# Narrow gate matmuls in four groups between the products of the next batch's first stage, and a wait per half ahead of the transposes

## The chip, the cores and the metric

The kernel runs on one core of one Trainium2 chip. The metric is the device time of one execution, in microseconds (us). The program has two parts on that core: an attention part over eight batches, and after it a mixture-of-experts part. The change touches the first part alone.

## The reference

Input `x` is 8 batches of 1024 rows of 256 values. In short:

```python
x = x + layernorm(attn(layernorm(x)))     # q, k, v from one projection; scores = q k^T / 4 over 1024 keys,
                                          # softmax, times v; out = swapaxes + reshape, then w_proj + bias
x = x + layernorm(ffn(layernorm(x)))
# ffn: logits = xn2 @ gate_w.T; scores = softmax(logits); top 1024 rows for each of 16 experts,
#      gated MLP of each expert (256 -> 1024 -> 256), weighted scatter-add, plus a shared MLP (256 -> 512 -> 256)
```

`xn2`, the second normalised rows, feeds the gate (16 logits for each row) as well as the experts.

## The kernel before

**Rounds.** The attention part is a loop over rounds r = 0 to 9, written out for each engine. Round r does the attention of batch r (r < 8), the output projection and first residual of batch r-1 (`R.post`, 1 to 8), and the gate of batch r-2 (`R.gate`, 2 to 9). Rounds 3 to 6 are a hardware loop; the others are written out. Each engine runs its own list in order, and semaphores couple them, so the written order is the order of the work.

**TensorE in a round.** The list of one round from 2 to 7 is:

1. Transposes of the normalised rows `XNB` of batch r-2 into the four PSUM banks of `psS` (L284). Sixteen of them, in four groups k = 0 to 3. Groups 0 and 1 read the rows of the first half (`ht` = 0, four tiles of 128 rows), groups 2 and 3 those of the second. Ahead of all of them stands one wait for both halves (`s_xn2`).
2. The output projection Y of batch r-1, 48 matmuls of 256 columns, 12 to a bank. It waits for the last `O_lo` of the round before (`s_ol`), and each bank for ScalarE's copy of its transposes (`s_n2`).
3. The gate's logits (L309): 16 calls of 16 columns, full fp32, which the trace shows as 32 matmuls, all into `psL`.
4. The first stage of batch r, in the code's name `tT`: x times the 256x256 matrix that joins the query and key weights. Four banks of six matmuls of 512 columns (three for each product, since operands are split into a high and a low part). One wait ahead of it asks for all four of VectorE's bias additions that empty the banks of Y (`s_yb`).
5. V (48 matmuls of 256 columns), and then eight steps of scores, transposes of the probabilities (L358) and outputs.

**ScalarE.** In the last step of a round it normalises tiles 4 to 7 into `XNB` (`norm_x1(r, range(4, 8))`, L391), and only then scales the last output tile (`O_hi`, L470), from which VectorE makes `O_lo` (L599). Tiles 0 to 3 are normalised one and two steps earlier. The half's semaphore `s_xn2` rises at tiles 3 and 7. At the start of the next round ScalarE copies the transposes (`xn2T`, L430).

**VectorE** adds the bias to Y (L522), then makes the low parts of `tT` and V, and then reads the logits (`gate_shift`, L538).

Of the kernel before, what the change touches and what calls it, by code (L numbers as in the profile page):

```python
# [31 lines left out]
NB, S, D = 8, 1024, 256  # L32
# [6 lines left out]
NT = S // P  # L39
# [9 lines left out]
def wait(eng, sem, value):  # L49

    if isinstance(value, int) and value <= 0:
        return
    eng.wait_ge(sem, value)


def mm3(pe, out, w_hi, w_lo, x_hi, x_lo, first, last):

    pe.matmul(out, w_hi, x_hi, start=first, stop=False)  # L58
    pe.matmul(out, w_hi, x_lo, start=False, stop=False)  # L59
    return pe.matmul(out, w_lo, x_hi, start=False, stop=last)  # L60
# [101 lines left out]
def attention(nc, io, c):  # L162
    with ExitStack() as ctx:
# [31 lines left out]
        s_y, s_yb = sem("s_y"), sem("s_yb")  # L195
        s_tr2, s_n2 = sem("s_tr2"), sem("s_n2")
        s_lg = sem("s_lg")
# [3 lines left out]
        s_pv, s_oh, s_ol = sem("s_pv"), sem("s_oh"), sem("s_ol")  # L201

        s_r1, s_xn, s_ry, s_yn, s_x1, s_r2, s_xn2 = (sem(n) for n in ("s_r1", "s_xn", "s_ry", "s_yn", "s_x1", "s_r2", "s_xn2"))
        s_sm, s_sme, s_sc = sem("s_sm"), sem("s_sme"), sem("s_sc")
# [4 lines left out]
        def output_bank(i):  # L209
            return (psO, psL)[i % 2][:, 0:D]  # L210
# [49 lines left out]
        def _(pe):  # L260
            def turn_x(b, ks):
                for k in ks:
                    dk, ht = k % 2, k // 2
                    if dk == 0:
                        wait(pe, s_xn, 2 * b + ht + 1)
                    for j in range(4):
                        i = pe.transpose(psS[:, k, j * P:(j + 1) * P], xn[:, 4 * ht + j, dk * P:(dk + 1) * P], c.ident[:, :])
                    i.then_inc(s_tr, 1)
# [6 lines left out]
            def body(R):  # L275
                r = R.r
                if R.gate:
                    wait(pe, s_xn2, 2 * (r - 1))
                    for k in range(4):
                        dk, ht = k % 2, k // 2  # L280
                        if R.attn:
                            wait(pe, s_xl, 4 * r + k + 1)
                        for j in range(4):
                            i = pe.transpose(psS[:, k, j * P:(j + 1) * P], XNB[:, 4 * ht + j, dk * P:(dk + 1) * P], c.ident[:, :])  # L284
                        i.then_inc(s_tr2, 1)
                if R.post:

                    wait(pe, s_ol, 8 * r)
                    for k in range(4):
# [5 lines left out]
                        for jj in range(2):  # L295
                            for q in range(2):
                                ot = 2 * (2 * jp + jj) + q
                                i = mm3(pe, psS[:, k, jj * D:(jj + 1) * D],
                                        O[0][:, ot, hm * P:(hm + 1) * P], O[1][:, ot, hm * P:(hm + 1) * P],
                                        c.wp[0][:, q, :], c.wp[1][:, q, :], q == 0, q == 1)  # L300
                        i.then_inc(s_y, 1)
                if R.gate:

                    wait(pe, s_n2, 4 * (r - 1))
                    wait(pe, s_sm, r - 2)
                    wait(pe, s_ol, 8 * r if R.attn else 8 * NB)
                    for t in range(NT):
                        for k in range(KD):
                            i = pe.matmul(psL[:, t * E:(t + 1) * E], xn2T[:, k, t * P:(t + 1) * P], c.gw[:, k, :],  # L309
                                          start=(k == 0), stop=(k == KD - 1))  # L310
                    i.then_inc(s_lg, 1)
                if R.attn:
                    wait(pe, s_xl, 4 * (r + 1))
                    if R.post:
                        wait(pe, s_yb, 4 * r)
                    for k in range(4):
                        m, h = k % 2, k // 2
                        for kk in range(KD):
                            w = [c.m[z][:, kk, m * P:(m + 1) * P] for z in (0, 1)]
                            x = [xnT[z][:, kk, h * 512:(h + 1) * 512] for z in (0, 1)]  # L320
                            i = mm3(pe, psS[:, k, :], w[0], w[1], x[0], x[1], kk == 0, kk == KD - 1)
                        i.then_inc(s_tt, 1)
                if R.attn:
                    for k in range(4):
                        wait(pe, s_tl, 4 * r + k + 1)
                        for t2 in range(2):
                            t = 2 * k + t2
                            for kk in range(KD):
                                w = [xnT[z][:, kk, t * P:(t + 1) * P] for z in (0, 1)]
                                i = mm3(pe, psS[:, k, t2 * D:(t2 + 1) * D], w[0], w[1],  # L330
                                        c.wv[0][:, kk, :], c.wv[1][:, kk, :], kk == 0, kk == KD - 1)
                        i.then_inc(s_v, 1)
                    for step in range(NT + 2):
                        i0, i1, i2 = step, step - 1, step - 2
                        if i0 < NT:
                            b = 2 * (i0 % 2)
                            if i0 < 2:
                                wait(pe, s_vl, 4 * r + 2 * i0 + 2)
                            else:
                                wait(pe, s_exp, 8 * r + i0 - 1)  # L340
                            for n in range(2):
                                for kk in range(KD):
                                    w = [tT[z][:, kk, i0 * P:(i0 + 1) * P] for z in (0, 1)]
                                    x = [xnT[z][:, kk, n * 512:(n + 1) * 512] for z in (0, 1)]
                                    i = mm3(pe, psS[:, b + n, :], w[0], w[1], x[0], x[1], kk == 0, kk == KD - 1)
                            i.then_inc(s_s, 1)
                        if R.ln_next and i0 >= NT:
                            if i0 == NT:
                                wait(pe, s_exp, 8 * r + 7)
                                turn_x(r + 1, (0, 1))  # L350
                            else:
                                wait(pe, s_exp, 8 * r + 8)
                                turn_x(r + 1, (2, 3))
                        def turn_p():
                            wait(pe, s_exp, 8 * r + i1 + 1)
                            wait(pe, s_ptl, 2 * (8 * r + i1))
                            for t in range(NT):
                                i = pe.transpose(psPT[:, t * P:(t + 1) * P], Pr[:, i1 % 2, t * P:(t + 1) * P], c.ident[:, :])  # L358
                                if t % 4 == 3:
                                    i.then_inc(s_t, 1)  # L360

                        def output(ts):
                            if ts[0] == 0:
                                wait(pe, s_ptl, 2 * (8 * r + i2 + 1))
                                wait(pe, s_ol, 8 * r + i2 - 1)
                                if i2 == 1 and R.gate:
                                    wait(pe, s_sm, r - 1)
                                if i2 == 0:
                                    wait(pe, s_vl, 4 * (r + 1))
                            for t in ts:  # L370
                                i = mm3(pe, output_bank(i2), PT[0][:, i2 % 2, t, :], PT[1][:, i2 % 2, t, :],
                                        V[0][:, t, :], V[1][:, t, :], t == 0, t == NT - 1)
                            if ts[-1] == NT - 1:
                                i.then_inc(s_pv, 1)

                        if i0 == NT:
                            output(range(NT // 2))
                            turn_p()
                            output(range(NT // 2, NT))
                        else:  # L380
                            if 0 <= i1 < NT:
                                turn_p()
                            if i2 >= 0:
                                output(range(NT))
            rounds(pe, body)

        @blk.scalar
# [1534 lines left out]
```

## Time and profile before

| | us |
|---|---|
| time before, median of 3 runs | 2126.94 (2126.02 to 2127.23) |
| the profiled execution's own time | 2126.23 |
| its span, first to last instruction | 2124.4 |
| TensorE matmul, busy | 2038.0 (96%) |
| VectorE, busy | 1194.5 (56%) |
| ScalarE, busy | 972.0 (46%) |
| mean granted TensorE clock | 0.981 |

Matmuls overlap one another in the trace: a matmul of 256 columns is shown with 0.28 us, and yet the next starts 0.12 us later. So lengths of stretches are read from start to start. "Idle before" in brackets is the time in which the engine had nothing under way.

### The profile page before, as it was taken

The page shows a single profiled execution, that of the slowest core. Times are in us where ns is not written, and L with a number is a line of the kernel's source. Part 1 is how long each engine was busy: PE and PEld are TensorE (multiplying, and loading weights), DVE is VectorE, ACT ScalarE, POOL GpSimd, SP SyncE. Part 2 cuts the span into 40 slices and gives each one's busy share as a digit, 9 for nine tenths or more (in the row PEclk, how much of TensorE's full clock was granted, in tenths as well). Part 3 has the DMA queues.
Part 4 walks back from the last instruction along what each step waited for, and adds up shares of the span by engine and source line. Part 5 has one row for each costly group of instructions (what it writes and reads, how often), then busy time and mean ns, then how long its engine had stood idle before and what let it go on. Part 6 is the DMA issues. An engine that isn't in the chain of part 4 may idle for free.

```text
span 2124.4 us, 32679 instructions
## 1 busy us (share of the span) xinstructions
PE 2038.0 (96%) x12590; PEld 1819.0 (86%) x12592; DVE 1194.5 (56%) x2518; ACT 972.0 (46%) x1809; POOL 436.3 (21%) x450
## 2 busy tenths in 40 slices
PE   7999999999994998999999999999999999999996
PEld 6899998998994887788888888888889898988885
DVE  5586686586564776555464546443443435353565
ACT  4464564564552433444343434344443434443443
POOL 0000000000001000212223222323233322322255
PEclk9999999999996999999999999999999999999998
DMA  3011110110014211233333333333333333334266
GB/s 112 1 41 42 60 62 41 59 60 41 40 42 159 102 60 42 69 91 91 61 91 62 91 64 88 64 89 71 83 79 77 76 80 84 69 91 100 53 193 132
DMA packets 55557, 159.91 MB, mean 75 GB/s; under 512 B 9473, under 2 KB 25985, under 8 KB 48257
## 3 DMA queue, kind: packets, MB, share of 16 engines
q1 hardware_dynamic: 28912, 116.16, 15.2%
q0 software_dynamic: 26512, 41.96, 12.4%
q8 instruction: 87, 1.43, 0.3%
q14 instruction: 46, 0.37, 0.1%
HBM read 98.78 MB, written 59.31 MB: 74 GB/s over the span
## 4 chain that ended last, share of the span: by engine, by line
PE 63%; DVE 2%; POOL 1%; ACT 1%; issue 1%; another core or an unknown queue 0%; DMA 0%; DVEq 0%; SPq 0%; ACTq 0%; POOLq 0%
PE mo_psD L58 7%; PE mo_psD L59 7%; PE mo_psD L60 7%; PE mo_psG L58 7%; PE mo_psU L60 7%; PE mo_psU L58 7%; PE mo_psG L59 7%; PE mo_psG L60 7%; PE mo_psU L59 7%; PE mo_psX L1210 1%; PE mo_psX L1026 1%; DVE mo_st L1502 0%; POOL mo_rs L1792 0%; DVE mo_HF L1538 0%
## 5 line engine op out<-in xcount | busy, mean ns | idle before, releaser
L1538 DVE TENSOR_TENSOR mo_HF<-mo_psU,mo_HF 128x512 f32<-128x512 f32 x320 | 221.0, 691 | 646.7 <-ACT mo_HF L1379 623.2
L1379 ACT ACTIVATE mo_HF<-mo_psG 128x512 f32<-128x512 f32 x320 | 191.2, 598 | 478.4 <-PE mo_psU L60 430.4
L1764 POOL DMA_INDIRECT ACC<-mo_OUT,mo_GI x128 | 202.9, 1585 | 700.1 <-ACT mo_OUT L1446 691.4
L60 PE MATMUL mo_psD<-mo_wd_hi,mo_H_lo 128*128 128x256 f32 x1024 | 289.8, 283 | 0.0
L59 PE MATMUL mo_psD<-mo_wd_lo,mo_H_hi 128*128 128x256 f32 x1024 | 289.8, 283 | 0.0
L58 PE MATMUL mo_psD<-mo_wd_hi,mo_H_hi 128*128 128x256 f32 x1024 | 289.6, 283 | 0.0
L1483 DVE TENSOR_TENSOR mo_H_lo<-mo_HF,mo_H_hi 128x512 fp32r<-128x512 f32 x300 | 204.3, 681 | 0.0
L1357 ACT ACTIVATE mo_H_hi<-mo_HF 128x512 fp32r<-128x512 f32 x320 | 199.7, 624 | 1.0 <-DVE mo_HF L1538 1.0
L59 PEld LDWEIGHTS mo_psD<-mo_wd_lo,mo_H_hi 128*128 128x128 f32 x1024 | 196.5, 192 | 1.2
L58 PEld LDWEIGHTS mo_psD<-mo_wd_hi,mo_H_hi 128*128 128x128 f32 x1024 | 196.5, 192 | 1.2
L60 PEld LDWEIGHTS mo_psD<-mo_wd_hi,mo_H_lo 128*128 128x128 f32 x1024 | 196.5, 192 | 0.0
L1446 ACT ACTIVATE mo_OUT<-mo_psD,mo_TW 128x256 f32<-128x256 f32 x128 | 60.7, 474 | 277.5 <-PE mo_psD L60 275.1
L654 POOL TENSOR_TENSOR X<-X,X1a 128x1024 f32 (+1 forms) x15 | 36.4, 2424 | 618.7 <-ACT X1a L391 618.7
L58 PE MATMUL mo_psG<-mo_XT_hi,wg_hi 128*128 128x512 f32 x344 | 140.3, 408 | 11.0 <-DVE mo_XT_lo L1478 11.0
L1753 POOL DMA_INDIRECT mo_XG<-XN,mo_GI x128 | 128.1, 1001 | 48.0 <-issue 34.1
L58 PE MATMUL mo_psU<-mo_XT_hi,wu_hi 128*128 128x512 f32 x344 | 135.4, 393 | 0.0
L59 PE MATMUL mo_psG<-mo_XT_lo,wg_hi 128*128 128x512 f32 x344 | 134.9, 392 | 0.0
L60 PE MATMUL mo_psG<-mo_XT_hi,wg_lo 128*128 128x512 f32 x344 | 134.7, 392 | 0.0
L60 PE MATMUL mo_psU<-mo_XT_hi,wu_lo 128*128 128x512 f32 x344 | 134.4, 391 | 0.0
L59 PE MATMUL mo_psU<-mo_XT_lo,wu_hi 128*128 128x512 f32 x344 | 134.4, 391 | 0.0
L58 PE MATMUL mo_psG<-mo_XT_hi,mo_wg_hi 128*128 128x512 f32 x280 | 113.0, 403 | 1.3 <-DVE mo_HF L1538 0.9
L59 PE MATMUL mo_psG<-mo_XT_lo,mo_wg_hi 128*128 128x512 f32 x280 | 109.3, 390 | 0.0
(262 smaller groups left out, 5183.3 us busy)
## 6 DMA issues: line engine op xcount, KB each, us to landing
X1a<-wg_in SPq DMA_DIRECT2D x16, 1024.0 KB, 4.9
X1a<-wu_in SPq DMA_DIRECT2D x16, 1024.0 KB, 4.9
X1a<-wd_in SPq DMA_DIRECT2D x16, 1024.0 KB, 4.9
XN<-XNB SPq DMA_DIRECT2D x8, 1088.0 KB, 4.1
X<-x_in SPq DMA_DIRECT2D x8, 1024.0 KB, 6.1
out_dram<-X SPq DMA_DIRECT2D x8, 1024.0 KB, 4.4
XN2T<-xn2T SPq DMA_DIRECT2D x8, 1024.0 KB, 3.8
mo_F<-ACC SPq DMA_DIRECT2D x7, 1024.0 KB, 12.8
```

The source lines that it names most:

```text
L58: pe.matmul(out, w_hi, x_hi, start=first, stop=False)
L59: pe.matmul(out, w_hi, x_lo, start=False, stop=False)
L60: return pe.matmul(out, w_lo, x_hi, start=False, stop=last)
L654: g.tensor_tensor(x, x, Y[:, 4 * h:4 * h + 4, :], ALU.add).then_inc(s_x1, 1)
L1026: i = pe.matmul(self.ps[:, 0, 0:SL * GE], self.lo1[:, t, :, :].rearrange("p v e -> p (v e)"), self.val[:, :, t * GE:(t + 1) * GE], start=( ...
L1357: a.activation(H[0][:, slot(b, it), :], HF[:, it % 2, :], ACT.Copy).then_inc(s_hhi, 1)
L1379: a.activation(HF[:, it % 2, :], psG[:, it % 2, :], ACT.Gelu).then_inc(s_gelu, 1)
L1446: a.activation(OUT[:, t, :], psD[:, t % 2, 0:D], ACT.Copy, scale=scale).then_inc(s_ev, 1)
L1483: v.tensor_tensor(H[1][:, z, :], HF[:, it % 2, :], H[0][:, z, :].bitcast(F32), ALU.subtract).then_inc(s_hlo, 1)
L1538: v.tensor_tensor(HF[:, it % 2, :], psU[:, it % 2, :], HF[:, it % 2, :], ALU.mult).then_inc(s_mul, 1)
L1753: g.indirect_dma_start(out=XG[q][:, t, :], out_offset=None, in_=io["XN"], in_offset=bass.IndirectOffsetOnAxis(ap=GI[q][:, t:t + 1], axis=0 ...
L1764: g.indirect_dma_start(out=io["ACC"], out_offset=bass.IndirectOffsetOnAxis(ap=GI[n % 2][:, 4 * tb + t:4 * tb + t + 1], axis=0), in_=OUT[:, ...
```

## The change

In rounds 2 to 7 the logits leave their place between Y and the first stage. They are issued in four groups of four calls (eight matmuls in the trace), one group behind each bank of the first stage. Their semaphores are waited for ahead of the first group, and `s_lg` rises behind the last. Rounds 8 and 9, which have no first stage, keep the logits in one piece.

The first stage waits for VectorE's bias additions bank by bank, in every round from 1 to 7. The transposes wait for `s_xn2` at each group: one half for groups 0 and 1, both for groups 2 and 3. In rounds 8 and 9 they wait for both halves as before.

```diff
@@ TensorE, body(R)
                 if R.gate:
-                    wait(pe, s_xn2, 2 * (r - 1))
                     for k in range(4):
                         dk, ht = k % 2, k // 2
+                        wait(pe, s_xn2, 2 * (r - 2) + ht + 1 if R.attn else 2 * (r - 1))
                         if R.attn:
                             wait(pe, s_xl, 4 * r + k + 1)
...
-                if R.gate:
-
-                    wait(pe, s_n2, 4 * (r - 1))
-                    wait(pe, s_sm, r - 2)
-                    wait(pe, s_ol, 8 * r if R.attn else 8 * NB)
-                    for t in range(NT):
+                def logits(ts):
+
+                    if ts[0] == 0:
+                        wait(pe, s_n2, 4 * (r - 1))
+                        wait(pe, s_sm, r - 2)
+                        wait(pe, s_ol, 8 * r if R.attn else 8 * NB)
+                    for t in ts:
                         for k in range(KD):
                             i = pe.matmul(psL[:, t * E:(t + 1) * E], xn2T[:, k, t * P:(t + 1) * P], c.gw[:, k, :],
                                           start=(k == 0), stop=(k == KD - 1))
-                    i.then_inc(s_lg, 1)
+                    if ts[-1] == NT - 1:
+                        i.then_inc(s_lg, 1)
+
+                if R.gate and not R.attn:
+                    logits(range(NT))
                 if R.attn:
                     wait(pe, s_xl, 4 * (r + 1))
-                    if R.post:
-                        wait(pe, s_yb, 4 * r)
                     for k in range(4):
                         m, h = k % 2, k // 2
+                        if R.post:
+                            wait(pe, s_yb, 4 * (r - 1) + k + 1)
                         for kk in range(KD):
                             w = [c.m[z][:, kk, m * P:(m + 1) * P] for z in (0, 1)]
                             x = [xnT[z][:, kk, h * 512:(h + 1) * 512] for z in (0, 1)]
                             i = mm3(pe, psS[:, k, :], w[0], w[1], x[0], x[1], kk == 0, kk == KD - 1)
                         i.then_inc(s_tt, 1)
+                        if R.gate:
+                            logits((2 * k, 2 * k + 1))
```

On TensorE, in the hardware loop (rounds 3 to 6), between the last matmuls of Y and the first stage, the program before has this. Each `psL<-gw,xn2T` row is a call of 16 columns, and `psS<-xnT_hi,m` the first stage.

```order
1319 L60 MATMUL psS<-wp,O_lo 128x256
1320 L53 REGISTER_ALU
1321 L309 MATMUL psL<-gw,xn2T 128x16 [waits s_ol,s_sm,s_n2]
1322 L309 MATMUL psL<-gw,xn2T 128x16 x15
1323 L53 ISA
1324 L58 MATMUL psS<-xnT_hi,m 128x512 [waits s_yb,s_xl]
1325 L59 MATMUL psS<-xnT_lo,m 128x512
```

The changed program has this in the same place.

```order
1323 L60 MATMUL psS<-wp,O_lo 128x256
1324 L53 ISA
1325 L53 ISA [waits s_xl]
1326 L58 MATMUL psS<-xnT_hi,m 128x512 [waits s_yb]
...
1331 L60 MATMUL psS<-xnT_hi,m 128x512
1332 L310 MATMUL psL<-gw,xn2T 128x16 [waits s_ol,s_sm,s_n2]
1333 L310 MATMUL psL<-gw,xn2T 128x16 x3
1334 L53 REGISTER_ALU
1335 L58 MATMUL psS<-xnT_hi,m 128x512 [waits s_yb]
...
1341 L310 MATMUL psL<-gw,xn2T 128x16 x4
1342 L53 REGISTER_ALU
1343 L58 MATMUL psS<-xnT_hi,m 128x512 [waits s_yb]
```

The sixteen calls that stood in a row ahead of the first stage are now four pieces, and the first stage follows on Y directly.

On TensorE, at the start of the loop's body, the transposes of `XNB` stand like this before.

```order
1255 L53 ISA [waits s_xn2]
1256 L284 MATMUL psS<-ident,XNB 128x128 [waits s_xl]
1257 L284 MATMUL psS<-ident,XNB 128x128 x3
1258 L53 REGISTER_ALU
1259 L284 MATMUL psS<-ident,XNB 128x128 [waits s_xl]
1260 L284 MATMUL psS<-ident,XNB 128x128 x3
```

And they stand like this in the changed program.

```order
1258 L53 ISA [waits s_xn2]
1259 L284 MATMUL psS<-ident,XNB 128x128 [waits s_xl]
1260 L284 MATMUL psS<-ident,XNB 128x128 x3
1261 L53 REGISTER_ALU [waits s_xn2]
1262 L284 MATMUL psS<-ident,XNB 128x128 [waits s_xl]
1263 L284 MATMUL psS<-ident,XNB 128x128 x3
1264 L53 REGISTER_ALU
1265 L53 REGISTER_ALU [waits s_xn2]
1266 L284 MATMUL psS<-ident,XNB 128x128 [waits s_xl]
```

The transposes keep their order, and the wait for `s_xn2` has gone from one to four, each with a register operation ahead of its group.

## Rows read from the trace of the kernel before

**Rows 1.** The page: busy time, and the granted clock in 40 equal slices.

```profile
PE 2038.0 (96%) x12590; PEld 1819.0 (86%) x12592; DVE 1194.5 (56%) x2518; ACT 972.0 (46%) x1809; POOL 436.3 (21%) x450
...
PEclk9999999999996999999999999999999999999998
```

**Rows 2.** TensorE's waits, 0 to 1000 us: total us, times, longest.

```profile
PE psS L284 <- ACT XNB L391: 21.9, 7, 18.1
...
PE mo_psG L58 <- DVE mo_XT_lo L1478: 11.0, 1, 11.0
...
PE psS L58 <- DVE X1a L522: 0.9, 1, 0.9
```

**Rows 3.** Stretches: busy of PE, PEld, DVE, ACT, POOL; granted clock; DMA.

```profile
250.60:254.00 3.40, 3.40 (x34) 3.40 (x32) 0.69 (x1) 0.00 (x0) 0.00 (x0) 1.00 0.02 5
254.90:258.10 3.20, 3.20 (x9) 2.52 (x8) 0.69 (x1) 0.60 (x1) 0.00 (x0) 0.50 0.00 0
...
910.20:913.50 3.30, 3.30 (x18) 3.30 (x17) 1.96 (x4) 0.38 (x1) 0.00 (x0) 0.50 0.00 0
```

**Rows 4.** Timeline, TensorE, round 3: start, length, instruction, idle before.

```profile
242.26 0.28 PE L60 MATMUL psL<-V_hi,PT_lo 128*128 128x256 f32 x1
243.03 1.96 PE L284 MATMUL psS<-ident,XNB 128*128 128x128 f32 x16 [0.49 <-ACT XNB L391]
244.75 0.36 PE L58 MATMUL psS<-wp,O_hi 128*128 128x256 f32 x1
...
250.59 3.64 PE L309 MATMUL psL<-gw,xn2T 128*128 128x16 f32 x32
254.08 0.47 PE L58 MATMUL psS<-xnT_hi,m 128*128 128x512 f32 x1
...
255.31 0.63 PE L59 MATMUL psS<-xnT_lo,m 128*128 128x512 f32 x1
255.74 0.63 PE L60 MATMUL psS<-xnT_hi,m 128*128 128x512 f32 x1
...
261.26 0.28 PE L58 MATMUL psS<-wv,xnT_hi 128*128 128x256 f32 x1
```

**Rows 5.** Timeline, TensorE, round 1, which has no gate.

```profile
96.96 0.28 PE L60 MATMUL psS<-wp,O_lo 128*128 128x256 f32 x1
98.11 0.47 PE L58 MATMUL psS<-xnT_hi,m 128*128 128x512 f32 x1 [0.87 <-DVE X1a L522]
98.42 0.40 PE L59 MATMUL psS<-xnT_lo,m 128*128 128x512 f32 x1
...
103.66 0.28 PE L58 MATMUL psS<-wv,xnT_hi 128*128 128x256 f32 x1
```

**Rows 6.** Timeline, TensorE, round 7: logits, and the start of V.

```profile
565.69 3.98 PE L309 MATMUL psL<-gw,xn2T 128*128 128x16 f32 x32
...
576.34 0.28 PE L58 MATMUL psS<-wv,xnT_hi 128*128 128x256 f32 x1
```

**Rows 7.** Timeline, TensorE, a score step: transposes of probabilities between wide matmuls.

```profile
355.15 1.04 PE L358 MATMUL psPT<-ident,Pr 128*128 128x128 f32 x8
355.94 0.36 PE L58 MATMUL psO<-V_hi,PT_hi 128*128 128x256 f32 x1
356.15 0.27 PE L59 MATMUL psO<-V_lo,PT_hi 128*128 128x256 f32 x1
```

**Rows 8.** Timeline, TensorE, start of round 5: last output, first transpose.

```profile
399.62 0.28 PE L60 MATMUL psL<-V_hi,PT_lo 128*128 128x256 f32 x1
400.65 0.54 PE L284 MATMUL psS<-ident,XNB 128*128 128x128 f32 x3 [0.75 <-ACT XNB L391]
```

**Rows 9.** Timeline, ScalarE, the same place.

```profile
398.49 2.03 ACT L391 ACTIVATE XNB<-X,shift,rs 128x256 f32 x4
400.43 0.45 ACT L470 ACTIVATE O_hi<-psL,rinv 128x256 fp32r<-128x256 f32 x1
```

**Rows 10.** Timeline, VectorE, the same place.

```profile
400.91 0.48 DVE L599 SCALAR_TENSOR_TENSOR O_lo<-psL,rinv,O_hi 128x256 fp32r<-128x256 f32 x1 [1.00 <-ACT O_hi L470]
```

## Prediction

> **What bounds the kernel now.** I read the page first: TensorE is busy 96% of the span and the next engine 56% [rows 1], so time can only come out of TensorE's own stretch, out of its pauses and out of its clock. Then TensorE's waits. Three of them lie where the change works or behind it: 21.9 us in seven pauses ahead of the transposes of `XNB`, of which 18.1 is one pause; and 0.9 us ahead of the first stage in round 1 [rows 2]. The pause of 18.1 is that of round 9, behind the last projection, where the code still waits for both halves; so the six rounds 2 to 7 share 3.8 us. The 11.0 us at the start of the expert part wait for a chain that begins when attention has ended [rows 2].
>
> Then the table of stretches, for the clock. In 250.60 to 254.00 TensorE is busy in every microsecond, with 34 matmuls, nearly all logits, and the clock is at its upper level (1.00, 2.4 GHz). In 254.90 to 258.10, at the start of the first stage, it is at the lower (0.50, 1.2 GHz) [rows 3]. The same table gives 0.50 right behind the logits in all six rounds 2 to 7, 78.5 us apart. The digits of the clock on the page are blind to it [rows 1]: a slice is 53 us long and such a low stretch a small part of it.
>
> Last, the timeline, from start to start. In round 3 the logits run from 250.59 to 254.08 (3.49 us) and the first stage from there to 261.26 (7.18 us), together 10.67. Low matmuls of 512 columns start 0.43 us apart (255.31, 255.74) [rows 4]. In round 1, which has no logits, the same 24 matmuls take from 98.11 to 103.66, 5.55 us, at the upper level [rows 5]. So 10.67 stand against 3.49 + 5.55 = 9.04: the fall costs 1.63 us a round. In round 7 the pair takes 576.34 - 565.69 = 10.65 [rows 6]; the other four lie between 10.63 and 10.67.
>
> **First part: the logits in four groups.** No instruction goes and none comes. What changes is how long TensorE does nothing but matmuls of 16 columns: 3.49 us in one piece before, four pieces of about 0.9 us with 1.4 us of wide matmuls (5.55 / 4) between them now. The reading is that the clock falls because for 3.4 us TensorE is busy with matmuls that stream hardly any columns. Two things in the trace speak for it: there is no pause ahead of the fall at all, and it comes only behind the logits, not behind the sixteen transposes of 128 columns (243.03 to 244.75), which have a real pause of 0.49 us in front of them [rows 4] and less narrow work in a row. A piece of 0.9 us is half of that transposing stretch, so I expect the upper level to hold. Gain: 6 x 1.63 = 9.8 us, less in rounds where a little of it is the switch below; I take 9.7. Its ends are 0 (the falls stay) and 9.8.
>
> The Trainium skill, "TensorE: Matmul & The Clock Gate", section "Why this matters for your kernels", advises against idle gaps between bursts of matmuls, since the clock goes back behind one. By that rule a stretch without a pause holds the upper level and the logits would have cost nothing; the trace shows the fall behind a stretch that is busy throughout [rows 3], so here the measurement decides.
>
> What does the splitting cost? A switch from narrow to wide delays the second wide matmul: 0.31 us from 98.11 to 98.42 where 0.23 is usual, so 0.08. Against that a group's first narrow matmuls come sooner. The nearest piece of the same size is that of eight transposes in a score step: 0.79 us until the next wide matmul, which is followed after 0.21 us instead of 0.12 [rows 7], so 0.88 for eight, 0.110 each. The logits in one piece cost 3.49 + 0.08 = 3.57 for 32, 0.112 each. Four groups of 0.88 are 3.52. I put the splitting at 0; its ends are -0.05 and, if every one of three new switches costs 0.08 with nothing given back, +0.25 a round, 1.5 us in all.
>
> **Second part: the bank's own bias wait.** In rounds 2 to 7 the logits covered the wait for the last bias addition (0.69 us of VectorE). Now the first stage follows on Y directly, but bank 0 needs only the first addition, three projections old (4.3 us), and bank 3 comes after three banks and three groups, some 6.8 us on. No wait is left. In round 1 there was no cover: last matmul of Y at 96.96, first stage at 98.11, where 97.08 would have been the next start. That is 1.03, and with the late second matmul 1.11 us [rows 5]. I take 1.1; ends 0.9 (the idle time alone) and 1.1.
>
> **Third part: the transposes.** In round 3 the last output matmul starts at 242.26 and the first transpose at 243.03, where 242.38 was due: 0.65 lost, shown as 0.49 idle [rows 4]. In round 5 it is 400.65 against 399.74: 0.91 [rows 8]. Idle time plus 0.16 is the loss, so the six rounds lose 3.8 + 6 x 0.16 = 4.8 us. Now groups 0 and 1 start at once, since the first half was normalised two steps earlier; they take half of 1.72, 0.86 us.
>
> What is late next? In round 5, the worst, ScalarE's rows end at 400.52 (398.49 + 2.03) and TensorE saw them at 400.65; groups 2 and 3 would be due at 399.74 + 0.86 = 400.60, so they start at 400.65 and end at 401.51 [rows 8, 9]. Y then waits for the last `O_lo`. `O_hi` stands behind those rows on ScalarE and ends at 400.88 [rows 9], `O_lo` ends at 401.39 [rows 10], and with the 0.13 us that TensorE took to see ScalarE's rows it may start at 401.52. Before, Y started at 400.65 + 1.72 = 402.37. So 0.85 of 0.91 comes back in rounds 4 to 6, and all of it in the other three, where the pause is shorter: 4.8 - 3 x 0.06 = 4.6 us. The two waits behind the one removed are level with it; were `O_lo` visibly later, it would cap this. Ends: 0 and 4.8.
>
> The added waits and their register operations stand in TensorE's queue, with everything of the round behind them. Y has four such waits now: its 48 matmuls take 250.59 - 244.75 = 5.84, which is 48 x 0.12 plus the 0.08 of the switch [rows 4]. So a wait that is already met costs 0.
>
> **Behind these places.** The last logits end 5.5 us later than before (9.04 - 3.49), but VectorE reads them only after the low parts of V, which end later still, so `gate_shift` doesn't wait. Rounds 8 and 9 are as before. Everything from there on hangs on the end of attention through TensorE, VectorE and DMAs in series, so what attention gains I pass on in full. The expert part has its own low stretches, behind its own pauses; one is 910.20 to 913.50 [rows 3]. Which matmuls such a stretch catches can shift with the start of the part, and I allow 1.6 us either way for each of two.
>
> **Sum.** 9.7 + 1.1 + 4.6 = 15.4 us. The profiled execution took 2126.2 us (span 2124.4 and 1.8 around it), so 2110.8. The median of the runs is 0.7 above that execution: 2111.5 us, 0.7% faster.
>
> **Rivals.**
>
> *The clock still falls in some or all rounds.* The narrow work is as much as ever, and over the stretch of 9 us it is still 40% of the time. For: nothing in the trace shows exactly this mix. Against: the score steps mix 0.8 us of transposes with wide work and stay up, though these have 128 columns and not 16. All six falls kept: 2126.9 - 1.1 - 4.6 = 2121.2; one to three kept: 2113 to 2116.4. Chance 15%.
>
> *Another wait takes the place of that for `XNB`.* `O_lo` is level with it to a few hundredths in round 5; if ScalarE's copies of the transposes or `O_lo` end later than read here, the 4.6 go: 2116.1. Chance 6%.
>
> *The slower end: each narrow group pulls the clock down, and the whole first stage runs at the lower level.* Place: the first stage of rounds 2 to 7. Price: 24 matmuls at 0.43 are 10.3 us instead of 5.55, with the narrow pieces 13.8 against 10.65 now, so +3.2 a round, +19.2, less the 5.7 of the other parts: 2140. It turns slower than before as soon as a round pays over 0.95 us (5.7 / 6) beyond today's fall. Against it stands that the wide matmuls between groups outlast the groups. Chance 4%.
>
> The Trainium skill, "TensorE: Matmul & The Clock Gate", section "A second HAM failure mode: psum-queue depth-cycling", speaks for this rival: frequent tiny pauses between groups made one kernel's clock swing back and forth. No row here shows it, and the score steps of this kernel with their short breaks don't.
>
> **How the numbers follow.** Forecast 75%, some falls kept 15%, the other wait 6%, slower 4%. A difference within 0.2% (4.3 us) is about what a measurement of this kernel can't tell from no change. All cases but the slower one, and a small part of the kept falls that adds up with another loss, end over 0.2% faster: faster 94%, same 3%, slower 3%. The range goes from 2107.5 (everything at its upper end, and both low stretches of the expert part gone) to 2118 (four falls kept, or the third part lost and one stretch of the expert part dearer).
>
> **What would show it.** Right: clock 1.00 throughout the rounds 2 to 7; logits and first stage together about 9.1 us in each; no pause ahead of the transposes over 0.1 us; no 0.87 us in round 1; the only large wait for `XNB` still that of 18 us. Wrong: 0.50 anywhere in a first stage, a new wait of Y for `O_lo` or `xn2T`, or gains that stand at the end of attention and are gone at the end of the span.

## The result

| | before | changed |
|---|---|---|
| median | 2127.09 us (4 runs, 2126.02 to 2128.38) | 2113.75 us (4 runs, 2111.77 to 2114.11) |
| profiled execution, own time | 2126.23 | 2114.11 |
| its span | 2124.4 | 2112.3 |
| ratio of the runs | | 0.9935, 95% interval 0.9918 to 0.9952 |

The changed kernel is 13.3 us faster by the medians, 12.1 us in the profiled pair. 2111.5 was forecast, in a range of 2107.5 to 2118.

### The profile page after: what moved, and what is told of

Its sections match the earlier page's. It is cut to its first block, busy times and chain, and to the rows that moved or that the text cites. A ratio compares the mean times of both kernels' runs of the same rounds, so it can differ in the third digit from the quotient of the medians.

```text
span 2112.3 us, 32697 instructions
## 1 busy us (share of the span) xinstructions
PE 2030.2 (96%) x12590; PEld 1814.4 (86%) x12592; DVE 1195.0 (57%) x2518; ACT 971.2 (46%) x1809; POOL 436.1 (21%) x450
## 3 DMA queue, kind: packets, MB, share of 16 engines
q1 hardware_dynamic: 28912, 116.16, 15.3%
## 4 chain that ended last, share of the span: by engine, by line
PE 64%; DVE 2%; issue 1%; POOL 1%; ACT 1%; DVEq 0%; another core or an unknown queue 0%; ACTq 0%; POOLq 0%
PE mo_psD L58 7%; PE mo_psD L60 7%; PE mo_psD L59 7%; PE mo_psG L58 7%; PE mo_psU L58 7%; PE mo_psG L59 7%; PE mo_psG L60 7%; PE mo_psU L60 7%; PE mo_psU L59 7%; PE mo_psX L1217 1%; PE mo_psX L1033 1%; DVE mo_st L1509 0%; POOL mo_rs L1799 0%; DVE mo_HF L1545 0%; DVE mo_XT_lo L1485 0%
```

## The profile after

The page of the changed kernel: busy time and the digits of the clock.

```profile
PE 2030.2 (96%) x12590; PEld 1814.4 (86%) x12592; DVE 1195.0 (57%) x2518; ACT 971.2 (46%) x1809; POOL 436.1 (21%) x450
...
PEclk8999999999995999999999999999999999999998
```

The same number of matmuls, 8 us less of busy time. As before [rows 1], the digits hide what happened in the rounds. The mean granted clock is 0.981 in both profiled executions, although six low stretches are gone; the reader should ask where others have come in. The stretches table of the changed kernel (busy of PE, PEld, DVE, ACT, POOL; clock; DMA) shows first two of the six stretches from the start of the first stage to V, then round 9's logits and the expert part's first matmuls.

```profile
170.60:179.60 9.00, 9.00 (x58) 7.95 (x57) 2.77 (x4) 2.38 (x4) 0.00 (x0) 1.00 0.00 0
247.30:256.30 9.00, 9.00 (x58) 7.96 (x56) 2.77 (x4) 2.37 (x4) 0.00 (x0) 1.00 0.01 2
...
654.10:657.50 3.40, 3.40 (x17) 3.40 (x17) 0.00 (x0) 0.00 (x0) 0.00 (x0) 0.50 0.73 308
657.50:660.80 3.30, 3.30 (x17) 3.30 (x16) 0.00 (x0) 0.00 (x0) 0.00 (x0) 0.50 0.00 0
672.00:675.90 3.90, 3.88 (x9) 3.11 (x10) 0.00 (x0) 0.46 (x1) 3.87 (x67) 0.50 1.08 414
```

The first two answer to [rows 3]: 1.00 where 0.50 stood, and the other four rounds read the same. The third and fourth are new in kind: all of round 9's logits at the lower level, 17 matmuls in 3.4 us against 34 in the same time at the upper [rows 3].

The second new place is the start of the program, ahead of everything that was changed. Round 0's first matmuls, before and then changed:

```profile
21.30:27.30 6.00, 6.00 (x17) 4.71 (x18) 0.82 (x2) 1.20 (x2) 0.00 (x0) 1.00 0.00 1
```

```profile
21.40:27.40 6.00, 6.00 (x14) 4.73 (x15) 0.69 (x1) 1.12 (x2) 0.00 (x0) 0.50 0.01 1
```

The changed kernel's timeline on TensorE in round 3 (start, length) is the answer to [rows 4].

```profile
239.66 0.28 PE L60 MATMUL psL<-V_hi,PT_lo 128*128 128x256 f32 x1
239.79 1.91 PE L284 MATMUL psS<-ident,XNB 128*128 128x128 f32 x16
241.45 0.36 PE L58 MATMUL psS<-wp,O_hi 128*128 128x256 f32 x1
...
247.29 0.40 PE L58 MATMUL psS<-xnT_hi,m 128*128 128x512 f32 x1
...
248.68 0.96 PE L310 MATMUL psL<-gw,xn2T 128*128 128x16 f32 x8
249.49 0.49 PE L58 MATMUL psS<-xnT_hi,m 128*128 128x512 f32 x1
249.81 0.40 PE L59 MATMUL psS<-xnT_lo,m 128*128 128x512 f32 x1
...
256.33 0.36 PE L58 MATMUL psS<-wv,xnT_hi 128*128 128x256 f32 x1
```

The transposes start 0.13 us behind the last output, without a pause. From the first stage to V it is 256.33 - 247.29 = 9.04 us, against 10.67. A group of eight takes 0.81 us to the next wide matmul, which is followed after 0.32.

In round 5 ScalarE's timeline

```profile
391.32 2.03 ACT L398 ACTIVATE XNB<-X,shift,rs 128x256 f32 x4
393.26 0.45 ACT L477 ACTIVATE O_hi<-psL,rinv 128x256 fp32r<-128x256 f32 x1
```

VectorE's

```profile
393.74 0.48 DVE L606 SCALAR_TENSOR_TENSOR O_lo<-psL,rinv,O_hi 128x256 fp32r<-128x256 f32 x1 [0.99 <-ACT O_hi L477]
```

and TensorE's

```profile
392.57 2.00 PE L284 MATMUL psS<-ident,XNB 128*128 128x128 f32 x16
394.36 0.38 PE L58 MATMUL psS<-wp,O_hi 128*128 128x256 f32 x1
```

answer to [rows 8 to 10]. `O_lo` ends at 394.22 (393.74 + 0.48) and Y starts at 394.36, 1.79 us behind the first transpose (1.66 in round 3). So rounds 4 to 6 still lose 0.13 us each, and round 7 loses 0.11. Read one by one, the transposes show where: the ninth, the first of group 2, starts 0.91 us behind the first instead of 0.87, and the tenth 0.16 behind the ninth instead of 0.11, so 0.08 us lie at the wait for the second half of `XNB`. The other 0.05 lie at Y, where `O_lo` is the last to come. Neither is long enough to stand in the list of waits.

TensorE's waits of [rows 2], 0 to 1000 us, total, times, longest:

```profile
PE psS L284 <- ACT XNB L398: 18.1, 1, 18.1
PE mo_psG L58 <- DVE mo_XT_lo L1485: 11.0, 1, 11.0
```

The six pauses for `XNB` and the one in round 1 are gone; what was left alone by the change is as long as before.

## The experiments

The first four runs shared a chip and the kernel before beside them, and so did the next four and runs nine to eleven. Run 12 had a fourth chip. Beside runs 5 to 8 and 12 the kernel before takes 2120 us instead of 2126 to 2127. The difference is in the expert part: from its first matmul to the end 1432 to 1433 us on those two chips and 1437 to 1442 on the others. So times are compared by their ratio to the kernel before on the same chip, and attention by the length from the first stage of round 1 to the start of round 8, which is 536.5 us before (634.58 - 98.11) and 522.7 changed (620.44 - 97.74).

### 1. The wait per half alone

```diff
 (kernel before)
                 if R.gate:
-                    wait(pe, s_xn2, 2 * (r - 1))
                     for k in range(4):
                         dk, ht = k % 2, k // 2
+                        wait(pe, s_xn2, 2 * (r - 2) + ht + 1 if R.attn else 2 * (r - 1))
```

> The kernel before with the third part alone (a wait per half ahead of the transposes). My theory: the parts add up, so this one gives its 4.6 us (2122.5 us), no pause over 0.1 us is left ahead of the transposes of rounds 2 to 7, Y starts 0.57 to 0.85 us sooner, and the six falls of the clock stay. Rival, the wait for O_lo takes its place: a new pause ahead of Y and about 2127.

Measured: 2119.0 us beside 2126.8, ratio 0.9966 (0.9952 to 0.9979), 7.8 us and not 4.6. No pause is left ahead of the transposes in its waits. The stretches just behind the logits of rounds 2 to 7 in its profile (the fifth reads the whole first stage of round 6):

```profile
171.90:175.10 3.20, 3.20 (x24) 2.99 (x25) 0.00 (x0) 0.00 (x0) 0.00 (x0) 1.00 0.00 0
250.40:253.40 3.00, 3.00 (x9) 2.50 (x9) 0.00 (x0) 0.00 (x0) 0.00 (x0) 0.50 0.00 0
328.90:331.90 3.00, 3.00 (x9) 2.32 (x8) 0.02 (x1) 0.60 (x1) 0.00 (x0) 0.50 0.00 0
407.40:410.40 3.00, 3.00 (x9) 2.35 (x8) 0.69 (x1) 0.60 (x1) 0.00 (x0) 0.50 0.00 0
482.00:490.00 8.00, 8.00 (x49) 7.02 (x49) 1.93 (x3) 1.79 (x3) 0.00 (x0) 1.00 0.00 0
561.00:564.00 3.00, 3.00 (x8) 2.32 (x8) 0.00 (x0) 0.42 (x1) 0.00 (x0) 0.50 0.00 0
```

Four falls instead of six. In rounds 2 and 6 logits and first stage take 9.06 us, in the others 10.62 to 10.67. Two falls less are 3.2 us, and 4.6 + 3.2 = 7.8. So the part's own gain was read rightly, and that it leaves the clock alone was not: with the same piece of logits but rounds of another length, fewer rounds fell. The rival (a wait for `O_lo` of the same size in its place) is out.

### 2. The bank's own bias wait alone

```diff
 (kernel before)
-                    if R.post:
-                        wait(pe, s_yb, 4 * r)
                     for k in range(4):
                         m, h = k % 2, k // 2
+                        if R.post:
+                            wait(pe, s_yb, 4 * (r - 1) + k + 1)
```

> The kernel before with the second part alone (the first stage waits for the bias additions bank by bank). My theory: it acts in round 1 alone, since the logits cover it elsewhere: 1.0 to 1.1 us (2126.0), the pause of 0.87 us gone, the six falls kept. Rival, it gives more because the first stage also waits in rounds 2 to 7: over 2 us.

Measured: 2126.61, ratio 1.0004 (0.9994 to 1.0013). No gain over all. In the profile the pause of round 1 is gone and the first stage there follows Y after 0.12 us, so 1.1 us were won; but three stretches of it, in rounds 2, 3 and 7, read

```profile
174.00:180.00 6.00, 6.00 (x18) 4.94 (x18) 0.69 (x1) 0.60 (x1) 0.00 (x0) 0.50 0.00 0
255.80:258.90 3.10, 3.10 (x9) 2.42 (x8) 0.69 (x1) 0.60 (x1) 0.00 (x0) 0.50 0.02 5
570.00:576.00 6.00, 6.00 (x16) 4.80 (x16) 0.69 (x1) 0.73 (x2) 0.00 (x0) 0.50 0.00 0
```

In rounds 2 and 7 the low stretch is twice as long and logits and first stage take 12.2 to 12.3 us. Its ten runs lie between 2124.5 and 2130.7, which is nearly four such stretches (6.2 us). While the falls exist, a gain of 1 us drowns in how many there are and how long. That the spread of the ten runs comes from them is likely and not shown, since only one of the ten was profiled.

### 3. The changed kernel with one wait for both halves

```diff
 (changed kernel)
                 if R.gate:
+                    wait(pe, s_xn2, 2 * (r - 1))
                     for k in range(4):
                         dk, ht = k % 2, k // 2
-                        wait(pe, s_xn2, 2 * (r - 2) + ht + 1 if R.attn else 2 * (r - 1))
```

> The changed kernel with the old single wait for both halves ahead of the transposes, so the logits in groups and the bank's own bias wait. My theory: 9.7 + 1.1 = 10.8 us off (2116.3), no fall of the clock in rounds 2 to 7, 3.8 us of waits for XNB back. Rival, the groups need the shorter pause ahead of the transposes to hold the clock: falls come back in some rounds, 1.6 us each, up to 2126.

Measured: 2115.51, ratio 0.9941 (0.9928 to 0.9955), 11.3 us off where 10.8 were expected. Its waits have the six pauses back

```profile
PE psS L284 <- ACT XNB L398: 3.8, 6, 0.8
```

and every round has 9.04 us from Y to V, no fall. Attention takes 527.2 us, 4.5 more than the changed kernel. So in the changed kernel the wait per half is worth 4.5 us, while alone it was worth 7.8: the two falls that it saves by itself are saved already.

### 4. The changed kernel with one wait for all bias additions

```diff
 (changed kernel)
                     wait(pe, s_xl, 4 * (r + 1))
+                    if R.post:
+                        wait(pe, s_yb, 4 * r)
                     for k in range(4):
                         m, h = k % 2, k // 2
-                        if R.post:
-                            wait(pe, s_yb, 4 * (r - 1) + k + 1)
```

> The changed kernel with the old wait for all four bias additions ahead of the first stage. My theory: with the logits gone from in front of it, the wait stands bare in all seven rounds 1 to 7, about 1.1 us each, so 7.7 us slower than the changed kernel (2121.5), with a pause of 0.87 us in each and the clock still up. Rival, only round 1 pays: 2114.9.

Measured: 2120.07 beside 2126.8, ratio 0.9967 (0.9955 to 0.9978), 6.3 us over the changed kernel's 2113.75 where 7.7 were expected. TensorE's waits, 0 to 640 us:

```profile
PE psS L58 <- DVE X1a L529: 6.1, 7, 0.9
```

Seven pauses of 0.87 us, and from the end of Y (0.12 us behind the start of its last matmul) to V 10.12 us instead of 9.04. The wait that the logits had covered costs 1.08 us a round as soon as they leave, 6.5 in rounds 2 to 7 (attention 529.2 us against 522.7), and with round 1 the expected 7.6; the rival is out. The clock stays up in all six rounds. Compared with experiment 1, which has the third part alone, this kernel has the groups on top and is no faster (0.9967 against 0.9966, attention 529.2 against 528.6): four falls saved, six bare waits paid. So the second part, which gained nothing measurable alone, is what makes the first one pay here.

### 5. Two groups instead of four

```diff
 (changed kernel)
-                        if R.gate:
-                            logits((2 * k, 2 * k + 1))
+                        if R.gate and k % 2 == 1:
+                            logits(range(4 * (k // 2), 4 * (k // 2) + 4))
```

> The changed kernel with the logits in two groups of eight calls (behind banks 1 and 3) instead of four of four. My theory: a piece of 1.8 us with 2.8 us of wide matmuls between still holds the upper level, so Y's end to V stays 9.04 us in each round and the time within noise of the changed kernel (2112 to 2115). Rival, four groups were needed: 0.50 in some first stages, 1.6 us each, 2117 or more.

Measured: 2104.98 beside 2120.32, ratio 0.9926 (0.9910 to 0.9941). The clock reads 1.00 in all six rounds, each piece takes 1.70 us to the next wide matmul, Y to V takes 9.02 us and attention 522.5 (522.7 with four groups). As good as four groups.

### 6. One piece, in another place

```diff
 (changed kernel)
-                        if R.gate:
-                            logits((2 * k, 2 * k + 1))
+                        if R.gate and k == 3:
+                            logits(range(NT))
```

> The changed kernel with all logits in one piece behind bank 3, ahead of V. My theory: the piece of 3.5 us pulls the clock down wherever it stands, now in V, in most of the rounds (four of six in the kernel before with the half wait alone), 1.6 us each: 2119 to 2123. Rival, what mattered was the place (the wait for the bias additions, the first stage's operands) and not the length of the piece: no fall, 2114.

Measured: 2110.02 beside 2120.32, ratio 0.9946 (0.9930 to 0.9961), 0.2% over the run before it. The stretches behind the logits of rounds 2, 3 and 4, which are in V now:

```profile
179.00:182.00 3.00, 3.00 (x16) 3.00 (x15) 0.18 (x1) 0.60 (x1) 0.00 (x0) 0.50 0.03 5
257.50:260.50 3.00, 3.00 (x16) 3.00 (x16) 0.69 (x1) 0.60 (x1) 0.00 (x0) 0.50 0.00 0
333.90:337.00 3.10, 3.10 (x28) 3.10 (x28) 0.20 (x1) 0.60 (x1) 0.00 (x0) 1.00 0.00 0
```

Rounds 2, 3, 5 and 6 fall, 4 and 7 don't, and attention takes 528.1 us, 5.4 more than changed. So the place is not what matters: in V too the clock falls behind the unbroken piece of 3.5 us. The number of falls came as expected. The time came out better, 10.3 us under the kernel before where 4 to 8 were expected; experiment 5 on the same chip is 15.3 under it too, where the changed kernel's own comparison has 13.3, and that difference stays unexplained.

### 7. Groups of double size

```diff
 (changed kernel)
-                    for t in ts:
+                    for t in [t for t in ts for _ in range(1 + bool(R.attn))]:
```

> The changed kernel with each logit call of rounds 2 to 7 issued twice in its group (the second overwrites the sum with a doubled one, so the logits are not the reference's). Groups of sixteen narrow matmuls with 1.4 us of wide ones between, narrow work 56% of the time over 12.6 us. If the clock holds: 32 more at 0.112 in six rounds, 21.5 us, 2135. My theory: it holds in some rounds and falls in others, 2137 to 2145. Rival, any alternation with wide work is enough: 2135 and no 0.50.

Measured: 2125.0 beside 2120.32, ratio 1.0020 (1.0010 to 1.0029). No fall, against what I expected; two rounds in its profile:

```profile
170.00:184.00 14.00, 14.00 (x101) 12.96 (x100) 3.46 (x5) 2.39 (x4) 0.00 (x0) 1.00 0.00 1
250.00:264.00 14.00, 14.00 (x101) 12.96 (x100) 3.46 (x5) 2.39 (x4) 0.00 (x0) 1.00 0.00 0
```

All six rounds take 12.62 us from Y to V, 3.58 more than 9.04, so 0.112 us for each of 32 more matmuls, and attention 21.4 us more. So in this run the clock held although narrow work took more than half of the time, in pieces of 1.70 us with 1.4 us of wide work between them. The expectation misread the edit in one point: both calls of a repeated pair are made again, the first with `start` set, so the sum begins anew and the logits are the same as before, not doubled. The work on TensorE is what was intended.

### 8. Wide matmuls in round 9's pause

```diff
 (changed kernel)
+                if R.gate and not R.attn and not R.post:
+                    for n in range(72):
+                        pe.matmul(psPT[:, 0:512], xnT[0][:, 0, 0:P], xnT[0][:, 0, 0:512], start=True, stop=True)
                 if R.gate:
```

> The changed kernel with 72 matmuls of 512 columns in round 9's pause of 18 us ahead of the last transposes (into a bank of which nothing is read), so that TensorE is not idle there. My theory: the last transposes and logits run at the upper level, 1.5 us and 3.1 us shorter where they ran low in the profiled execution; all of it goes to the start of the expert part: 2109 to 2111, and less spread between runs. Rival, the chain to the expert part goes through DMAs and not through the logits: no change.

Measured: 2102.93 beside 2120.32, ratio 0.9916 (0.9902 to 0.9929). The last transposes and the last logits:

```profile
650.40:653.00 2.60, 1.87 (x17) 1.63 (x15) 0.00 (x0) 1.92 (x4) 0.00 (x0) 1.00 0.00 0
653.20:656.60 3.40, 3.40 (x31) 3.40 (x31) 0.00 (x0) 0.00 (x0) 0.00 (x0) 1.00 0.73 308
```

Upper level; transposes to logits 2.8 us instead of 4.4, logits 3.5 instead of 6.6 in the changed kernel's profile (start to start). From the start of round 8 to the first matmul of the expert part it takes 48.2 us instead of 51.6, although the 72 matmuls outlasted the pause by 1.4 us. The chain goes through the logits; the rival is out.

### 9. The changed kernel again

> The changed kernel once more, beside the next two on one chip, since the last four runs had another chip than the first five. Against the kernel before: ratio 0.9935 as before, within 0.9918 to 0.9952, and attention without a fall of the clock.

Measured: 2111.15 beside 2126.45, ratio 0.9929 (0.9915 to 0.9943), attention 522.7 us, no fall. Here the last logits took 4.1 us and the start of round 8 to the expert part 50.0 us instead of 51.6.

### 10 to 12. Both pauses filled, and an earlier load

```diff
 (changed kernel; 60 matmuls ahead of round 9's transposes, and n more here: 34, 30, 14)
                 if R.gate and not R.attn:
                     logits(range(NT))
+                if R.gate and not R.attn and not R.post:
+                    for n in range(34):
+                        pe.matmul(psPT[:, 0:512], xnT[0][:, 0, 0:P], xnT[0][:, 0, 0:512], start=True, stop=True)
...
 (SyncE, in 11 and 12)
+                if R.post and not R.attn:
+                    sp.wait_ge(s_xtst, 16)
+                    sp.dma_start(c.XR0[:, :, :], io["XN2T"][0][:, :, 0:512]).then_inc(c.s_xr0, 16)
...
-            sp.dma_start(c.XR0[:, :, :], io["XN2T"][0][:, :, 0:512]).then_inc(c.s_xr0, 16)
```

> The changed kernel with 60 wide matmuls in round 9's pause (72 outlasted it by 1.4 us in the last trial) and 34 more behind the last logits, ahead of the expert part. My theory: 4 to 6 us under the changed kernel from round 9, and another 2 to 3 us because the expert part's first twenty-four matmuls (5.2 us for the first twelve at the lower level) start at the upper one. Rival, the pause of some 3 us between the parts lets the clock fall all the same: only the first gain.

> The same (30 matmuls in the second place) with the load of XR0, which ends the attention part, issued in round 8 instead of behind the last store of XN. My theory: the barrier to the expert part then waits for that store alone, which landed 4.8 us after its issue where the load took until 6.1 us after it: 1.3 to 2 us less. Rival, the expert part's start hangs on something else: no change against the run beside it.

> The last kernel with 14 matmuls instead of 30 behind the last logits. In it SyncE was done at 663.8 us and the barrier between the parts still came at 666.5, because TensorE was working off the 30. My theory: the barrier now comes 2 to 2.7 us sooner, the expert part's first matmuls may run at the lower level (about 1.5 us back), and the sum is 0.5 to 2.5 us under the last two: ratio 0.991. Rival, the last run's gain was not hidden by these matmuls: same time or slower.

Measured: run 10, 2109.72 beside 2126.45, ratio 0.9922 (0.9909 to 0.9936); run 11, 2109.64, ratio 0.9920 (0.9906 to 0.9933); run 12, on its own chip, 2102.02 beside 2120.39, ratio 0.9915 (0.9901 to 0.9928). In run 10 the last logits and the expert part's first twelve matmuls read

```profile
651.90:653.60 1.70, 1.70 (x16) 1.70 (x16) 0.00 (x0) 0.00 (x0) 0.00 (x0) 1.00 0.62 265
653.80:656.70 2.90, 2.90 (x15) 2.90 (x16) 0.00 (x0) 0.00 (x0) 0.00 (x0) 0.50 0.43 181
669.00:671.80 2.80, 2.80 (x12) 2.34 (x13) 0.00 (x0) 0.42 (x1) 2.80 (x55) 1.00 1.04 398
```

The second filling did its work here (2.9 us for twelve, against 4.9 in run 9 and 5.2 in the kernel before), the first only in part: half way through the logits the clock is at the lower level. Run 10 is 1.4 us under run 9 by the medians, not the 6 us and more expected. In run 11, where 1.3 to 2 us more were expected and 0.1 measured, SyncE's waits show why the early load gave nothing:

```profile
SPq L258 <- DMA XN<-XNB: 3.7, 1, 3.7
SPq L163 <- PEq L163: 2.5, 1, 2.5
```

The store that is left made SyncE wait 3.7 us, and then SyncE stood 2.5 us at the barrier for TensorE, which was working off the 30 matmuls. The filling also missed its other aim there: with 30 matmuls instead of 34 the expert part's first twelve ran at the lower level again (clock 0.50 from 668.60 to 671.80) and took 4.3 us. With 14 (run 12) the start of round 8 to the expert part takes 45.6 us, against 48.6 in run 11 and 51.6 in the changed kernel's first profile. Runs 11 and 12 differ in nothing but these 16 matmuls, so that the barrier waited for them is shown. Run 12 has the lowest ratio of all, but its interval overlaps that of the changed kernel; that it is faster over all is likely and not settled.

## Why the prediction was right

**The mechanism and its size held.** First part: 9.04 us in each of six rounds against 10.63 to 10.67, 9.7 us, as forecast. Experiment 3 shows it without the third part; experiments 5 and 6 show that the length of the unbroken piece does it and not its place. Second part: 98.11 - 96.96 = 1.15 us in round 1 became 0.12, and the delayed second matmul went too: 1.1 us, as forecast. Third part: pause and transposes together became 0.6 to 0.8 us shorter in each round, 4.6 us in all, as forecast, and as read from [rows 8 to 10] the second half of `XNB` and `O_lo` came nearly level with the transposes: they still cost 0.08 and 0.05 us in the worst rounds.

**The splitting was mis-sized, within its bounds.** It was put at 0. V now stands behind narrow work: its 48 take 5.84 us instead of 5.75, so 0.09 in six rounds, 0.5 us.

**Two terms were missing, both outside the changed places.** The sum of the parts is 15.4 - 0.5 = 14.9 us, and round 8 starts 14.1 us sooner (620.44 against 634.58). Of the difference 0.7 us comes from the program's start: Y of round 1 begins 0.66 us later (91.89 against 91.23) ahead of anything that was changed, and 0.56 of it is round 0's first stage, 8.40 us with the lower level at its start instead of 7.84. And then 2.8 us were lost between round 9's logits and the expert part: 15.20 us from the first of these logits to the first expert matmul before, 18.00 changed. The prediction put rounds 8 and 9 "as before" and allowed only for the expert part's low stretches, 1.6 us either way for each of two; those came to 0.8 us in favour (1441.1 us before, 1440.3 changed). The larger term was round 9's logits, in one piece behind a pause of 18 us, which before ran mostly at the upper level. The stretch there, in the kernel before:

```profile
668.10:671.10 3.00, 2.97 (x27) 2.97 (x27) 0.00 (x0) 0.00 (x0) 0.00 (x0) 1.00 0.72 306
```

That is not a fixed cost of the change: run 9, the same kernel, has 15.5 us in that place, and experiment 2 (which has no group) has 18.0. Of the ten profiles with nothing added in round 9, three show 18.0 (the changed kernel, experiments 2 and 6) and seven 15.0 to 15.7. With the 15.2 of the kernel before the profiled execution would have taken 2111.3 us; 2110.8 was forecast for it. Run 9 stands at 2111.15, 15.3 us under the kernel before beside it. So part of the miss of 2.2 us in the median may be in which level these logits met; only one of the first four runs was profiled.

**The additive reading was wrong in one place.** The parts were priced apart and summed. In the sum this was harmless, since all three are made; taken alone they don't behave so (7.8, 0 and, for the first with the old bias wait, 6 x 1.08 us of it eaten). The tacit step that failed is that six falls come with the piece of 3.5 us: with the same piece and rounds of another length there were four (experiment 1). The groups alone, with both old waits, were not run.

**The rivals.** No fall stayed. The slower rival got nothing: groups of 8, of 16, and of 16 with half the wide work between them all read 1.00. Its price was too low as well. It let the narrow pieces keep their 3.5 us at the lower level, where round 9's logits took 6.6 (the same 32 matmuls), so such a round would have cost some 6 us more and not 3.2. The Trainium skill, "TensorE: Matmul & The Clock Gate", section "A second HAM failure mode: psum-queue depth-cycling", tells of tiny idle times between groups of matmuls; the groups here left none (busy 9.00 us of 9.00), so no run here tests it.

**What stays open.** What picks the rounds that fall, when one unbroken piece stands in each (four of six in experiments 1 and 6, all six before, and all six in experiment 2, two of them twice as long), was not tried further. Nor was it tried what in these matmuls does it: that they have only 16 columns was argued, and no run has an equally long piece of other matmuls. The four runs of the changed kernel differ by 2.3 us; from round 9's logits to the expert part the profiles differ by 3.0 (15.0 to 18.0), but which runs had which was not seen.

## What to carry to other kernels

Look for the clock in stretches of a few microseconds right behind narrow work, not in the page's digits: a stretch can be busy throughout and still be followed by wide matmuls at half speed. Breaking the narrow piece with wide work that is there anyway cost almost nothing here (under 0.1 us a round), but whatever the piece was hiding (here 1.08 us a round of bias additions) must get a finer wait in the same edit. Judge such an edit whole: two of its parts, taken alone, measured 7.8 and 0 us, where they are worth 4.5 and some 7.5 in the whole.

## What the runs showed of the hardware

- Narrow matmuls run at half pace at the lower level too: 17 logits matmuls in 3.4 us, 34 at the upper, though they stream only 16 columns each.
- The clock fell behind an unbroken 3.5 us of such matmuls with TensorE busy all the time, in 20 of 24 rounds (the kernel before, experiments 1, 2 and 6), and behind pieces of up to 1.7 us with 1.4 us or more of wide matmuls between them in none of 60 (the changed kernel, experiments 3 to 5 and 7 to 12).
- Of four chips two ran the kernel before in 2126 to 2127 us and two in 2120. The expert part shows the difference (1437 to 1442 us against 1432 to 1433); the attention of the changed kernel doesn't (522.7 in run 9, 522.6 in run 8).
- Sixteen transposes of 128 columns start 0.11 us apart at the upper level and 0.21 at the lower (round 9 of the changed kernel).
